# Four graph layers on one core: another sorting network with ranges of its own, six weight fills in place of nine, a shallower maximum tree, and new instruction orders

## The reference

```
h_mod = [x_i, x_j] @ W_pre + b_pre                       # layer 0, for every edge (i, j)
m = [mean_j, max_j, min_j, std_j of h_mod over members]
x = LN(x + [x, m, m*log_deg/4.86, m*4.86/log_deg] @ W_post + b_post)
x = LN(x + adj @ (x @ W) + bias)                         # layer 1
adj_d = adj without every skip-th neighbour of rows with more than 10 of them
agg = 0.25*q(0.25) + 0.5*q(0.5) + 0.25*q(0.75)           # quantiles of x over the members of a row
x = LN(x + (relu((x + agg) @ W1 + b1) @ W2 + b2) * mask) # layer 2
x = LN(x + ((adj + I) @ x) / (deg + 1))                  # layer 3
```

## Time and profile before

| | us |
|---|---|
| median of 3 runs | 722.21 |
| the profiled execution | 724.17 |
| its span (first to last instruction) | 722.0 |
| DVE busy | 571.4 (79%) |
| PE busy | 538.8 (75%) |
| ACT busy | 365.4 (51%) |
| POOL busy | 142.3 (20%) |
| mean granted TensorE clock | 0.797 |

### The profile page before, as it was taken

One profiled execution on the slowest core, in us unless ns is written; L12 is line 12 of the kernel. 1 busy time (PEld: TensorE's weight loads), 2 busy tenths in 40 slices (PEclk: granted clock), 3 DMA queues, 4 the chain that ended last, 5 costly groups with the idle time before them and its releaser, 6 DMA issues.

```text
span 722.0 us, 10480 instructions
## 1 busy us (share of the span) xinstructions
PE 538.8 (75%) x3419; PEld 349.9 (48%) x3419; DVE 571.4 (79%) x1530; ACT 365.4 (51%) x982; POOL 142.3 (20%) x211
## 2 busy tenths in 40 slices
PE   2559759977897799779978897879977995880520
PEld 2534744555556455655556454645554553540220
DVE  4995567998979988998799879997999789659421
ACT  1356375546662776267636665475727652250040
POOL 4400050001033202420061006100611041005013
PEclk9659975999798968997899779986999597555555
DMA  8200110020000200020002000200000000000000
GB/s 325 96 1 1 31 42 1 2 73 1 2 8 8 74 1 5 11 74 1 1 15 74 2 1 16 74 1 1 15 2 1 1 12 4 0 1 15 0 2 16
DMA packets 6570, 18.26 MB, mean 25 GB/s; under 512 B 1648, under 2 KB 1776, under 8 KB 6000
## 3 DMA queue, kind: packets, MB, share of 16 engines
q1 hardware_dynamic: 4464, 15.44, 6.1%
q0 software_dynamic: 2048, 2.10, 0.9%
HBM read 15.44 MB, written 2.10 MB: 24 GB/s over the span
## 4 chain that ended last, share of the span: by engine, by line
DVE 33%; PE 27%; issue 25%; ACT 7%; POOL 5%; DVEq 0%; POOLq 0%; ACTq 0%
PE ring L401 9%; DVE slot L1360 7%; PE pna L401 6%; POOL out_dram L1058 4%; DVE slot L1426 4%; PE rest L404 3%; DVE slot L1443 2%; DVE hot L1426 2%; PE ring L611 2%; PE ring L404 2%; PE pna L404 2%; ACT wv L809 1%; PE relab L401 1%; DVE deg L1102 1%; DVE hot L1326 1%
## 5 line engine op out<-in xcount | busy, mean ns | idle before, releaser
L401 PE MATMUL ring<-hot,parts 128*128 128x328 bf16 (+3 forms) x768 | 167.6, 434 | 4.8 <-DVE hot L1326 4.8
L1058 POOL DMA_INDIRECT out_dram<-xo,idx x64 | 76.8, 1201 | 325.7 <-DVE xo L1393 308.7
L858 ACT ACTIVATE slot<-ring 128x512 f32<-128x512 f32 (+1 forms) x128 | 62.9, 525 | 55.0 <-PE ring L401 49.8
L401 PEld LDWEIGHTS ring<-hot,parts 128*128 128x128 bf16 (+1 forms) x768 | 61.5, 123 | 53.4 <-issue 15.6
L809 ACT ACTIVATE wv<-pna,rowP 128x64 f32<-128x64 f32 x128 | 27.9, 329 | 100.4 <-PE pna L401 100.4
L1360 DVE TENSOR_TENSOR slot<-slot 128x128 f32<-128x128 f32 (+2 forms) x144 | 70.0, 504 | 8.4 <-ACT slot L858 5.7
L1426 DVE TENSOR_TENSOR slot<-slot,hot 128x512 f32<-128x512 f32 (+3 forms) x120 | 60.1, 512 | 0.8
L404 PE MATMUL ring<-emp,rowsel 112*128 112x512 bf16 (+1 forms) x128 | 47.5, 371 | 9.4 <-issue 5.4
L404 PE MATMUL ring<-sgnT,delta 32*128 32x512 bf16 (+5 forms) x72 | 21.9, 336 | 38.4 <-DVE slot L1434 38.2
L867 ACT ACTIVATE slot<-ring 128x384 f32<-128x384 f32 x64 | 32.1, 508 | 31.1 <-PE ring L401 30.9
L1426 DVE TENSOR_TENSOR hot<-hot,slot 128x64 f32<-128x64 f32 (+4 forms) x120 | 47.0, 414 | 0.5
(11 more groups left out here) (284 smaller groups left out, 1203.5 us busy)
## 6 DMA issues: line engine op xcount, KB each, us to landing
Cc<-adj_cols_dram SPq DMA_DIRECT2D x8, 512.0 KB, 3.8
R<-adj_rows_dram SPq DMA_DIRECT2D x8, 512.0 KB, 4.7
slot<-adj_rows_dram SPq DMA_DIRECT2D x4, 1024.0 KB, 12.1
xn<-x_nat_dram SPq DMA_DIRECT2D x8, 256.0 KB, 4.7
out_dram<-xo,idx POOLq DMA_INDIRECT x64, 2.3
weights<-wpack_dram SPq DMA_DIRECT2D x1, 608.5 KB, 8.1
biasr<-wrows_dram SPq DMA_DIRECT2D x1, 128.0 KB, 9.0
mask<-node_mask_dram SPq DMA_DIRECT2D x1, 8.0 KB, 4.7
```

Source lines behind the costliest of these rows:

```text
L401: return mm(*a, start=False, stop=True, skip_group_check=True, **k)
L858: A(slot0[:, g, lo:hi], PG[ring["g0", t.n, 2 * g + j][0]][:, 0:hi - lo], ACT.Copy).then_inc(s["slot0"], 1)
L1058: nc.gpsimd.indirect_dma_start(out=out, out_offset=bass.IndirectOffsetOnAxis(ap=idx[t.n % ROWKEEP][:, g:g + 1], axis=0), in_=xo[:, g, :], ...
```

## The change

1. The sorting network is another one, of 34 compares in place of 35, written as a flat list. For each compare the range is worked out by member count: a rank r is wanted only in rows whose count can use it (`RCAP`: 128 columns for ranks 0 to 3, 72 for 4, 48, 32, 16, 16 in place of 96, 72, 48, 32, 16 for ranks 4 to 8), and a compare runs over the widest class that needs its result. `plan_sort` then lists the 66 instructions (68 before) so that an instruction does not stand right behind the one whose result it needs, and gives each its own wait.
2. The weights of ranks 5 to 8 share one `ring` buffer: six fills (`WFILLS`) in place of nine. `wg` multiplies four ranks after the last fill. `ag` sums in pairs, and rank 4's sum goes straight into `x2T`.
3. `tr` folds in pairs as a tree: column groups 8 to 11, 5 with 6, 7 with 12 are independent. The ten widths are the same.
4. In `yl` the product with `bdx` opens the PSUM bank and the bias is added over 2x64 columns, in place of 2x192 first. Three small copies at the start fall into the loop above them.
5. All order tables but SyncE's entries are new. `va`, `p2` go into the middle of `g2` (before: behind `g0:0` and `g0:3`), `cr` behind `g0:1`, `dt` ahead of `ss`, `c2:1` right behind `c2:0`; on ScalarE `vt`, `k2` move up likewise, `sg` behind `e0:2`. On GpSimd `pb` for the next group stands ahead of the stores. On VectorE 28 of the sort's steps stand ahead of `xo`'s scaling (33 before), 16 between it and `zf:0` (10), 22 between the two `zf` (22 and `nb`), none behind (3), and `wg:0`, `wg:1` come ahead of `zf:1`.

```diff
+RCAP = [max(CAP2[m - 1] for m in range(1, K2 + 1) if any(abs(r - tau * (m - 1)) < 1 for tau in TAUS))
+        for r in range(RANKS)]
+WFILLS = ((0,), (1,), (2,), (3,), (4,), (5, 6, 7, 8))
...
+def pair(todo, j, k):
+    return todo[j][1:5] == todo[k][1:5] and not todo[j][0] and todo[k][0] and todo[j][5] >= todo[k][5]
...
+    classes = sorted(set(CAP2))
+    lows, highs = [0] * len(NETWORK), [0] * len(NETWORK)
+    for c in classes:
+        live = {r for r in range(RANKS) if RCAP[r] >= c}
+        for k in reversed(range(len(NETWORK))):
+            a, b = NETWORK[k]
+            if CAP2[b] < c:
+                continue
+            if a in live:
+                lows[k] = c
+            if b in live:
+                highs[k] = c
+            if a in live or b in live:
+                live |= {a, b}
...
+    while len(place) < len(todo):
+        ready = [k for k in range(len(todo)) if k not in place and all(j in place for j in after[k])]
+        best = max(ready, key=lambda k: (all(place[j] < len(place) - 1 or pair(todo, j, k) for j in after[k]), depth[k]))
+        hard = [place[j] for j in after[best] if not pair(todo, j, best)]
+        steps.append(todo[best] + (max(hard, default=None),))
+        place[best] = len(place)
...
 TENSOR_ORDER = """
+    g0:1@-1 cr@-1 g0:2@-1 g0:3@-1 kc@0 g0:4@-1 lv@0 g0:5@-1 g0:6@-1 g0:7@-1 yl:0@-1 wr:0@-2 wr:1@-2 yr@0 yl:1@-1
...
-                    new(both, rows3[:, :], biasb[:, 1, 0:6 * D].rearrange("p (a w) -> p a w", a=2))
-                    add(both, xT[:, c, :], bdx[:, :, :])
+                    new(both, xT[:, c, :], bdx[:, :, :])
+                    add(both[:, :, 0:D], rows3[:, :], biasb[:, 1, 0:2 * D].rearrange("p (a d) -> p a d", a=2))
...
-                new(PG[which][:, 0:PAIRS * CAP2[r]], delta[:, r, :, :].rearrange("p a d -> p (a d)"),
-                    sgnT[t.n % KEEP][:, :, 0:CAP2[r]]).then_inc(s["w_ps"], 1)
+                at = 0
+                for r in WFILLS[f]:
+                    done = new(PG[which][:, at:at + PAIRS * RCAP[r]], delta[:, r, :, :].rearrange("p a d -> p (a d)"),
+                               sgnT[t.n % KEEP][:, :, 0:RCAP[r]]) if at == 0 else add(
...
-                mark("narrow", fold(slot0[:, half, OFF0[8]:OFF0[10]], slot0[:, half, OFF0[10]:OFF0[12]]))
+                mark("eight", fold(slot0[:, half, OFF0[8]:OFF0[10]], slot0[:, half, OFF0[10]:OFF0[12]]))
+                mark("five", fold(at(5, CAP0[6]), at(6, CAP0[6])))
+                mark("seven", fold(at(7, CAP0[12]), at(12, CAP0[12])))
...
-                    elif steps[k - 1][0] != layer:
-                        need("sort")
-                    low, high = wire(a, sa, CAP2[b]), wire(b, sb_, CAP2[b])
+                    if needs is not None:
+                        need(("sort", needs))
+                    low, high = wire(a, sa, width), wire(b, sb_, width)
...
+                need("four")
+                mark("total", take("total", 4))
+                need("total")
+                take("total", 0).then_inc(s["o2T"], 1)
```

More of the change, by code:

```diff
@@ new lines, in plan_sort @@
+    depth = [0] * len(todo)
+    for k in reversed(range(len(todo))):
+        for j in after[k]:
+            depth[j] = max(depth[j], depth[k] + PAIRS * todo[k][5] + 200)
+    place = {}
+    while len(place) < len(todo):
[4 more added lines that the diff above has]
+        place[best] = len(place)
@@ new lines, in take @@
+                def take(what, r):
+                    at = total[:, :, 0:RCAP[r]]
+                    return V.tensor_tensor(at, at, ranked(r), ALU.add)
+                fold("seven", 7, 8)
+                fold("five", 5, 6)
+                fold("zero", 0, 1)
+                need("seven")
+                fold("four", 4, 7)
+                fold("two", 2, 3)
+                need("four")
+                need("five")
+                fold("four", 4, 5)
+                need("two")
+                fold("zero", 0, 2)
```

148 lines of the change are left out of this document (75 added, 73 removed), and 11 rows, old and new, of the table NETWORK.

## The result

The changed kernel takes **672.4 us** (median of 4 runs, 671.0 to 673.9); the kernel before took 723.3 beside it. The ratio is 0.931, 95% interval 0.927 to 0.935. I had forecast 704, range 690 to 717: the sign was right, the gain came out at 51 us in place of 18.

A forecast was written before the change was run, and what follows sets the result against it. No engine is full: VectorE and TensorE take turns, legs of 49.3 and 25.9 us per 75.2 us period. Six periods at 1.6 (9.6), start 2.5, end 3.9 and 2.6 save 18.6 us: 704 us against the median, range 690 to 717.

The forecast's parts named there:

- C: Last piece of the TensorE leg, from the sort's first step to the reciprocal ahead of `xo`; not forecast separately.
- TensorE leg: From the last `hot2` to the reciprocal ahead of `xo`, 25.9 us; forecast 1.0 us longer per period (0 to +2).
- VectorE leg: From the reciprocal ahead of `xo` round to the last `hot2`, 49.3 us; forecast 2.6 us shorter per period.
- B: First piece of the TensorE leg, from the last `hot2` to the sort's first step; not forecast separately.
- A: Window name of the VectorE leg, from the reciprocal ahead of `xo` to the last `hot2`.
- spacing: VectorE instructions no longer right behind one they need: 0.12 us each; per group 0.8 in the sort, 0.95 in the tree.
- Start: Before the repeating periods: one tree and half a sort on the path, 2.5 us less.
- End: Last group's sort, `wg` and `ag` run bare, 3.9 us less; before it the previous group's second half, 2.6 less.
- All comes through: Rival: all of VectorE's saving counts, the TensorE leg does not grow; 4.2 us per period, 688 us; chance 0.12.
- The clock rival: Rival: TensorE's low clock stretch grows by 10 us per period, making the kernel slower, 733 us; chance 0.07.
- The waits rival: Rival: sort steps' already met semaphore waits cost 0.12 us each, some 4 us per period; 735 us; chance 0.05.
- taken back: Rival: the TensorE leg grows 2.6 us, cancelling the VectorE leg's gain; only start and end gain; 715 us; chance 0.16.

The follow-up runs named there:

- experiment 3: Changed kernel with `va` and `p2` (and ScalarE's copies `vt`, `k2`) back where they stood in the orders: 684.3 us, 0.945.
- experiment 4: Five sort steps moved between A and C in VectorE's order: out of C in the kernel before, 740.1 us; into C in the changed kernel, 673.0.
- experiment 1: The change in two halves, against the kernel before: new steps with old orders 691.7 us (0.957), old steps with new orders 713.0 us (0.989).
- experiment 5: Only `va`, `p2`, their copies, `dt`, its copy and `dr` moved: on the kernel before 738.8 us; on new steps with old orders 703.7 to 715.6.
- Experiment 2: Kernel before with overwritten filler products on TensorE in each group: 14 products 718.0 us (0.992), 21 products 715.6 us (0.991).
- experiment 6: Changed kernel with one part undone at a time: old sort network and planner 694.4 us, old tree 675.5, nine weight fills 669.2.

## Why the prediction was wrong

I take the sum apart by the time of the reciprocal ahead of `xo`: of the first group (207.3 before, 197.4 after), of the seventh (653.45 and 603.03, the ends of the last C in the windows), and the span (722.0 and 669.3).

- **Six periods: forecast -9.6, measured -40.5.** Of the 31 us between, 25 are the TensorE leg and 6 the VectorE leg. The step that failed is the TensorE leg. I wrote that it gets 1.0 longer in each period; in the five middle ones it got 3.5 shorter. In it B behaved: +1.3 for my +1.0. But I had priced `va` and `p2` at the low clock, and B ran at the full one, so that agreement is partly luck. C fell by 4.8, and I had no term for it. I had treated B and C as one leg with one bound. TensorE's 17.36 of 17.40 us busy was my reason that it "can't go faster", and that row itself said 0.51: half speed. Busy at half the clock is no floor.
- What made the leg shorter can be read from experiment 3: B and C together are 26.2 us at the low clock and 20.9 at the full one, and 22.4 with `va` and `p2` among the fills. So the clock gives 5.2 and the move takes 1.4, for 25.9 before and 22.4 after. C alone got shorter by the clock (3.3), by `va` leaving it for B (1.8), and by fewer sort steps, which count only once TensorE no longer bounds C (experiment 4). These overlap: C cannot go below its VectorE work of 9.36.
- That the new orders keep the clock up in B and C is shown by the two halves of experiment 1 and by experiment 5. Why is not settled. In the changed kernel the 12.9 us ahead of the last `hot2` are as thin as before (TensorE busy for 9.1 in both); there, in the period shown, the clock fell inside them and was up again by B; in the kernel before it stayed up through them and fell with B. Experiment 2 speaks against the simplest answer, gaps.
- **VectorE leg: forecast -2.6, measured -3.5.** VectorE's work in A fell by 2.3 us (46.54 to 44.27), so the widths and the spacing were right in size (experiment 6: 2.4 for 2.7, 0.7 for 0.95). The other 1.2 is less waiting in A, which I had no term for. The windows show that A waits less only with the steps and the orders together (46.2 with 42.0 of work for the steps alone, 52.7 with 48.7 for the orders alone); why is not taken apart here.
- **Start: forecast -2.5, measured -9.9.** New steps alone took 7.1 off it, new orders alone 7.4. I had counted one tree and half a sort. The last `hot2` of the first group comes at 105.7 in place of 111.5 (104.9 with the new orders alone, 110.2 with the new steps alone), the second group's follows it 1.5 us closer, and from there to the reciprocal it is 2.4 less. I had no term for the orders in the start; which entries give the 5.9 at its head these runs don't tell.
- **End: forecast -6.5, measured -2.3 behind the seventh reciprocal.** The two are not cut at one place: 2.6 of the forecast lie in the sixth period, which got 5.6 shorter (its B was at 1.2 GHz before and after, 15.07 and 15.08), and another part in its C (10.79 to 9.36). From the sort's first step to the end of the last sum it was 34.3 us and is 29.7, from 593.67 to this row: 4.6 less, for my 3.9. What follows got 0.9 longer, behind the last `xo`.

```profile
622.66 0.69 DVE L1501 TENSOR_TENSOR x2T<-x2T,slot 128x512 f32<-128x512 f32 x1
```

- **The rivals.** "All comes through" (688) was right that the TensorE leg does not grow, for a reason I had ruled out. The clock rival had the right cause with the wrong sign: I asked what a longer low stretch would cost and never what a shorter one would give, though the same row prices both. The waits rival fell at once. Two of the rivals' sums were off: "taken back" comes to 714 by my own terms, not 715, and +11 for the clock rival adds the 5 us to the forecast's -1.6 and does not put them in its place, as the text says.

By the sentence on chaining that the prediction took from the Trainium skill ("VectorE: DVE Perf Modes", section "The DRAIN you can't avoid") the spacing terms would be worth nothing. The old tree, with the same widths and only other dependences, costs 0.7 us more work per group (44.98 against 44.27), so here the measurement decides against it, as the earlier trace rows did. The prediction read that section too narrowly: it also says that a next instruction which is not held (made to wait for all earlier ones to finish) starts earlier, and with that the 0.60 us between the starts of 0.69 us instructions agree.

## What to carry to other kernels

A row that shows an engine full at clock 0.5 names a bound that can halve, so price both a longer and a shorter low stretch before you call it a floor. A low stretch costs most where TensorE is the bound: 5.2 us for 10 us of it in B and C, 0.6 for 7 us of it in A. Cut a leg at every wait where the bound can change hands; work is free only in the piece where another engine is the bound, and moving it across such a border is a cheap test of who that is. A saving on one engine is worth its own size only while the others keep their clock: here 2.6 us of VectorE work in A came with up to 14 us more of low clock, and A was 3.4 to 5.7 us longer (experiment 6).
